# A hybrid convolution, attention and expert layer on one core: who scales the value rows, who sums the first norm, and in which order the head weights come

## The reference

```python
q, k = Wq @ x + bq, Wk @ x + bk           # 16 rows each
v = Wv @ x + bv                           # 128 rows
x = gamma * (v @ softmax(q.T @ k / 4).T) + x

t = tokens(x)
h = layernorm(t) @ qkv_w + qkv_b          # 8 heads, q and v of 128 each
attn = sum_n(q[:, n]) * sum_r(lunchbox)   # what the einsums come to, per head
t = t + (attn * v) @ proj_w + proj_b

t = t + moe(layernorm(t))                 # 8 experts, the best two of each token
```

## Time and profile before

| What | Value |
|---|---|
| Median of 3 executions | 491.35 us (491.24 to 493.74) |
| The profiled execution | 488.81 us |
| Its span, first to last instruction | 487.0 us |
| TensorE busy | 425.6 us, 87% |
| TensorE weight loads | 368.3 us, 76% |
| VectorE busy | 310.4 us, 64% |
| ScalarE busy | 197.5 us, 41% |
| GpSimd busy | 157.7 us, 32% |
| Mean granted clock of TensorE | 0.939 |

### The profile page before, as it was taken

One profiled execution on the slowest core, in us unless ns is written; L12 is line 12 of the kernel. 1 busy time (PEld: TensorE's weight loads), 2 busy tenths in 40 slices (PEclk: granted clock), 3 DMA queues, 4 the chain that ended last, 5 costly groups with the idle time before them and its releaser, 6 DMA issues.

```text
span 487.0 us, 9131 instructions
## 1 busy us (share of the span) xinstructions
PE 425.6 (87%) x2833; PEld 368.3 (76%) x2833; DVE 310.4 (64%) x834; ACT 197.5 (41%) x386; POOL 157.7 (32%) x163
## 2 busy tenths in 40 slices
PE   5989899999899988999879969986987999999825
PEld 2569567996669976778867969885876899999813
DVE  6855887458985589877667756744434455555425
ACT  4070534614337244163138336634333344444403
POOL 1020000010024440134517834455565444444510
PEclk9599999999999999999969979989899999999955
DMA  7090000100000200002103101123222222222159
GB/s 221 0 297 22 1 0 1 45 2 0 1 17 24 73 23 1 11 12 101 39 14 110 46 12 51 54 71 84 67 67 62 60 64 67 62 62 68 39 185 344
DMA packets 23621, 30.20 MB, mean 62 GB/s; under 512 B 5074, under 2 KB 16978, under 8 KB 23448
## 3 DMA queue, kind: packets, MB, share of 16 engines
q1 hardware_dynamic: 19256, 20.63, 14.2%
q0 software_dynamic: 4320, 8.99, 5.5%
HBM read 17.44 MB, written 12.16 MB: 61 GB/s over the span
## 4 chain that ended last, share of the span: by engine, by line
PE 60%; DVE 23%; issue 8%; ACT 5%; DMA 2%; POOL 0%; SPq 0%; another core or an unknown queue 0%; DVEq 0%; POOLq 0%; ACTq 0%
PE bank_c L393 27%; PE bank_s L393 21%; PE bank_c L592 4%; PE bank_a L393 4%; DVE row_max_sb L975 3%; DVE values_sb L1041 2%; DVE probs_sb L1422 2%; ACT probs_sb L804 2%; PE bank_a L571 1%; DVE ln_sb L1013 1%; DVE qk_sum_sb L1215 1%; DMA probs_sb<-y_dram 1%; DVE lnT_lo_sb L1210 1%; DVE qk_hi_sb L1220 1%; PE bank_a L464 1%
## 5 line engine op out<-in xcount | busy, mean ns | idle before, releaser
L1492 POOL DMA_INDIRECT y_dram<-probs_sb x71 | 68.2, 961 | 86.9 <-ACT probs_sb L914 84.3
L1447 POOL DMA_INDIRECT xs_dram<-ln_rows_sb,slots_sb x64 | 67.3, 1052 | 86.6 <-issue 57.4
L393 PE MATMUL bank_c<-v_ext_sb,probs_sb 128*128 128x129 f32 x512 | 61.4, 275 | 1.8 <-DVE t_sb L998 1.6
L847 ACT ACTIVATE values_sb<-bank_s,g_head_sb 128x1024 fp32r<-128x1024 f32 x32 | 35.1, 1113 | 66.0 <-PE bank_s L393 52.5
L393 PEld LDWEIGHTS bank_c<-v_ext_sb,probs_sb 128*128 128x128 f32 x512 | 59.4, 191 | 3.0 <-DVE t_sb L998 1.2
L393 PE MATMUL bank_s<-probs_sb,lnT_hi_sb 128*128 x142 | 52.9, 373 | 1.9 <-issue 1.3
L393 PE MATMUL bank_c<-values_sb,wp_hi_sb 128*128 128x256 f32 x256 | 53.8, 288 | 0.0
L1439 POOL TENSOR_TENSOR rstd_sb<-var_eps_sb,minus_half_sb 128x4 f32<-128x4 f32 x16 | 16.5, 1029 | 102.4 <-DVE var_eps_sb L1007 102.4
L1215 DVE TENSOR_TENSOR qk_sum_sb<-v_ext_sb,bank_s 128x341 f32<-128x341 f32 x35 | 17.8, 510 | 49.5 <-ACT v_ext_sb L903 31.9
L393 PE MATMUL bank_s<-w_rest_sb,lnT_hi_sb 128*128 x142 | 46.6, 328 | 0.0
L393 PE MATMUL bank_s<-probs_sb,lnT_lo_sb 128*128 x142 | 46.4, 327 | 0.0
(11 more groups left out here) (197 smaller groups left out, 899.5 us busy)
## 6 DMA issues: line engine op xcount, KB each, us to landing
probs_sb<-xs_dram SPq DMA_DIRECT2D x71, 66.0 KB
probs_sb<-y_dram SPq DMA_DIRECT2D x16, 256.0 KB, 6.7
w_rest_sb<-in_w_dram SPq DMA_DIRECT2D x1, 2728.0 KB, 13.8
xc_sb<-in_x_dram SPq DMA_DIRECT2D x4, 512.0 KB, 3.6
y_dram<-probs_sb POOLq DMA_INDIRECT x71
xs_dram<-ln_rows_sb,slots_sb POOLq DMA_INDIRECT x64
xs_dram<-pads_sb SPq DMA_DIRECT2D x1, 528.0 KB, 7.4
xs_dram<-pads_sb SPq DMA_DIRECT2D x8, 66.0 KB
```

The lines of the kernel that those rows point to most:

```text
L393: return nc.tensor.matmul(bank, lhsT, rhs, start=start, stop=stop)
L847: nc.scalar.activation(vh_hi[:, hd % RING, :], bank_s[hd % 2][:, :], ACT.Copy, scale=g_head[:, hd:hd + 1]).then_inc(vh_high, 1)
L1447: G.indirect_dma_start(xs_dram, bass.IndirectOffsetOnAxis(ap=slots[:, i, k:k + 1], axis=0), ln2x(i)[:, k // TILES, k % TILES, :], None).th ...
L1492: G.indirect_dma_start(y_dram, bass.IndirectOffsetOnAxis(ap=x_rows[k][:, C:C + 1].bitcast(I32), axis=0), y_rows[k], None).then_inc(scatter ...
```

## The change

It does four things. The value rows of images 1 to 3 are kept by ScalarE, which multiplies by gamma alone; their bias is added by TensorE, as one more matmul per half at the head of the accumulation, from 32 rows of the bias split into high and low parts (`bv_rows`) against rows that hold 1/16 (`shares`). The sum of the norm over tokens is made by TensorE: each of the eight tiles of normed rows stands as the stationary operand against a column of ones of `v_ext`, accumulated in one column of `bank_s[1]`, from which ScalarE copies it; the two accumulating reads of ScalarE go, and a bank `Cb` is drained by VectorE's low part. TensorE's `head_sums` stands ahead of head values 0, with one column where there were two, and VectorE's head weights stand between the query stack and the key stack, with three operations for four. Four small operations of VectorE are added ahead of the loop.

```diff
@@ TensorE
             def project_v(i, h):
+                if i == 1:
+                    pe.wait_ge(consts_made, 9)
                 pe.wait_ge(A[h].drained, A[h].before(i, "v"))
+                mm(bank_a[h][:, :], shares[BIAS_ROWS, :], bv_rows[BIAS_ROWS, :].unsqueeze(1).broadcast_to([2 * DQK, 4, C]), stop=False)
                 for j in range(4):
                     n = 4 * h + j
-                    last = mm(bank_a[h][:, j * C:(j + 1) * C], xc[:, n * P:(n + 1) * P], wvT_s[:])
+                    last = mm(bank_a[h][:, j * C:(j + 1) * C], xc[:, n * P:(n + 1) * P], wvT_s[:], start=False, stop=(j == 3))
                 last.then_inc(A[h].filled, 1)
...
+            def sum_ln1(i, h):
+                if h == 0:
+                    pe.wait_ge(S[1].drained, S[1].before(i, "sum"))
+                for n in range(4 * h, 4 * h + 4):
+                    last = mm(bank_s[1][:, 0:1], ln1[:, n, :], v_ext[:, 0, C:VCOLS], start=(n == 0), stop=(n == TILES - 1))
+                if h == 1:
+                    last.then_inc(S[1].filled, 1)
+
             def head_sums(i):
 
-                for h in range(2):
-                    pe.wait_ge(Cb[h].drained, Cb[h].after(i, "ln1"))
+                pe.wait_ge(S[1].drained, S[1].after(i, "sum"))
+                pe.wait_ge(Cb[0].drained, Cb[0].after(i, "ln1"))
                 for hd in range(HEADS):
-                    last = mm(bank_c[0][:, 2 * hd:2 * hd + 2], wq_s[:, hd * P:(hd + 1) * P], ln1_sum[:, :])
+                    last = mm(bank_c[0][:, hd:hd + 1], wq_s[:, hd * P:(hd + 1) * P], ln1_sum[:, :])
...
                     if hd == 0 and n == 2:
-                        pe.wait_ge(lnT_low, 2 * i + 2)
+                        for c in Cb:
+                            pe.wait_ge(c.drained, c.after(i, "ln1"))
...
                 turn_ln1(i, 0)
+                sum_ln1(i, 0)
                 if not last:
                     project_v(i + 1, 0)
                 if not first:
                     rank(i - 1)
                 turn_ln1(i, 1)
+                sum_ln1(i, 1)
                 if not last:
                     project_v(i + 1, 1)
...
+                head_sums(i)
                 head_values(i, 0)
-                head_sums(i)
                 head_values(i, 1)
@@ ScalarE
-                for h in range(2):
-                    act.wait_ge(lnT_low, 2 * i + h + 1)
-                    nc.scalar.activation(lnT[:, h * HALF:(h + 1) * HALF], bank_c[h][:, :], ACT.Identity,
-                                         accum_out=ln1_sum[:, h:h + 1]).then_inc(Cb[h].drained, 1)
+                act.wait_ge(S[1].filled, S[1].full(i, "sum"))
+                nc.scalar.copy(ln1_sum[:], bank_s[1][:, 0:1]).then_inc(S[1].drained, 1)
+
+            def keep_v(i):
+                for h in range(2):
+                    act.wait_ge(A[h].filled, A[h].full(i, "v"))
+                    nc.scalar.activation(v_ext[:, 4 * h:4 * h + 4, 0:C], bank_a[h][:, :].rearrange("p (n c) -> p n c", c=C),
+                                         ACT.Copy, scale=vec_s[:, 1:2]).then_inc(A[h].drained, 1)
...
                 keep_ln1T(i)
+                if not last:
+                    keep_v(i + 1)
                 keep_head_values(i)
@@ VectorE
             def head_weights(i):
                 s0 = i * G_STEPS
                 dve.wait_ge(Cb[0].filled, Cb[0].full(i, "qsum"))
-                V.tensor_reduce(qsum[:], bank_c[0][:, 0:2 * HEADS].rearrange("p (h t) -> p h t", t=2), AX_X, ALU.add).then_inc(Cb[0].drained, 1)
+                V.tensor_tensor(qsum[:], bank_c[0][:, 0:HEADS], nbq[:], ALU.add).then_inc(Cb[0].drained, 1)
                 dve.wait_ge(Cb[0].drained, Cb[0].after(i, "qsum"))
-                step(V.tensor_tensor(qsum[:], qsum[:], nbq[:], ALU.add), g_step, s0, 1)
-                step(V.tensor_scalar(g_head[:], qsum[:], lunch_sum[:, 0:1], None, ALU.mult), g_step, s0, 2)
+                step(V.tensor_scalar(g_head[:], qsum[:], lunch_sum[:, 0:1], None, ALU.mult), g_step, s0, 1)
...
-                    make_stacks(i + 1)
+                    make_stacks(i + 1, [QUERIES])
                 head_weights(i)
                 if not last:
-                    keep_v(i + 1)
+                    make_stacks(i + 1, [KEYS])
...
+            bv_hi = t1[BIAS_ROWS, TILES - 1, :].bitcast(F32R)
+            V.tensor_copy(bv_hi, bvB_s[BIAS_ROWS, :]).then_inc(setup, 1)
+            V.memset(shares[BIAS_ROWS, :].bitcast(F32), 1.0 / DQK).then_inc(consts_made, 1)
+            dve.wait_ge(setup, 5)
+            V.scalar_tensor_tensor(out=bv_rows[BIAS_ROWS, :], in0=bv_hi.bitcast(F32),
+                                   scalar=cst_s[BIAS_ROWS, C_LOW:C_LOW + 1],
+                                   in1=bvB_s[BIAS_ROWS, :],
+                                   op0=ALU.mult, op1=ALU.add).then_inc(consts_made, 1)
```

More of the change, by code:

```diff
@@ L124, in conv_attn_moe_kernel @@
         gbv = sb("gbv", [P, C])
+        BIAS_ROWS = slice(STACK, STACK + 2 * DQK)
+        bv_rows = sb("bv_rows", [P, C], F32R)
+        shares = sb("shares", [P, P], F32R)
         v_ext = sb("v_ext", [P, TILES, VCOLS])
@@ L147, in by_stride @@
             return half[:].rearrange("c (k p) -> c p k", k=HEADS)[:, h * (P // 2):(h + 1) * (P // 2), :]
-        ln1_sum = sb("ln1_sum", [P, 2])
+        ln1_sum = sb("ln1_sum", [P, 1])
         nbq = sb("nbq", [P, HEADS])
@@ L247, in order_s @@
             for i in range(IMAGES):
-                order += [("rank", i - 1, 0)] * (i > 0 and b == 0) + [("vh", i, k) for k in range(HEADS // 2)]
+                order += [("rank", i - 1, 0)] * (i > 0 and b == 0) + [("sum", i, 0)] * (b == 1) + [("vh", i, k) for k in range(HEADS // 2)]
                 if i + 1 < IMAGES:
@@ L277, in conv_attn_moe_kernel @@
         setup, den_ready, tok_step = sem("setup"), sem("den_ready"), sem("tok_step")
-        heads_made, vh_high, lnT_high, lnT_low = sem("heads_made"), sem("vh_high"), sem("lnT_high"), sem("lnT_low")
+        heads_made, vh_high, lnT_high = sem("heads_made"), sem("vh_high"), sem("lnT_high")
         qk_high, wv_low = sem("qk_high"), sem("wv_low")
         wv_high, g_step, bias_ready = sem("wv_high"), sem("g_step"), sem("bias_ready")
-        G_STEPS = 3
+        G_STEPS = 2
         tables_ready, table_step, hidden_cleared = sem("tables_ready"), sem("table_step"), sem("hidden_cleared")
@@ L836, in keep_ln1T @@
                     nc.scalar.copy(by_stride(lnT_hi, h), bank_c[h][:, :].rearrange("c (p k) -> c p k", k=HEADS)).then_inc(lnT_high, 1)
+                act.wait_ge(S[1].filled, S[1].full(i, "sum"))
+                nc.scalar.copy(ln1_sum[:], bank_s[1][:, 0:1]).then_inc(S[1].drained, 1)
+            def keep_v(i):
                 for h in range(2):
[L838 to L840 removed]
+                    act.wait_ge(A[h].filled, A[h].full(i, "v"))
+                    nc.scalar.activation(v_ext[:, 4 * h:4 * h + 4, 0:C], bank_a[h][:, :].rearrange("p (n c) -> p n c", c=C),
+                                         ACT.Copy, scale=vec_s[:, 1:2]).then_inc(A[h].drained, 1)
             def keep_head_values(i):
[L843 removed]
+                act.wait_ge(g_step, i * G_STEPS + 1)
                 for hd in range(HEADS):
@@ L956, in bcast_e, with make_stacks @@
                 return ap.unsqueeze(2).broadcast_to([P, TILES, EXPERTS])
-            def make_stacks(i):
+            QUERIES, KEYS = (q_stack, 0), (k_stack, STACK)
+            def make_stacks(i, stacks):
                 for h in range(2):
                     dve.wait_ge(A[h].drained, A[h].after(i, "qk"))
-                for k, (dst, lo) in enumerate(((q_stack, 0), (k_stack, STACK))):
+                for dst, lo in stacks:
                     rows = slice(lo, lo + STACK)
@@ L964, in make_stacks @@
                                            in1=qk_sum[rows, :], op0=ALU.mult, op1=ALU.add).then_inc(stack_step, 1)
-            def keep_v(i):
-                for h in range(2):
[L968 to L971, removed]
             def keep_max(i, n):
@@ L1035, in low_lnT @@
                     V.tensor_tensor(by_stride(lnT_lo, h), bank_c[h][:, :].rearrange("c (p k) -> c p k", k=HEADS),
-                                    by_stride(lnT_hi, h).bitcast(F32), ALU.subtract).then_inc(lnT_low, 1)
+                                    by_stride(lnT_hi, h).bitcast(F32), ALU.subtract).then_inc(Cb[h].drained, 1)
             def low_head_values(i, hd):
@@ L1350, in _ @@
             dve.wait_ge(qk_high, 2)
-            make_stacks(0)
+            make_stacks(0, [QUERIES, KEYS])
             for n in range(TILES):
```

## The result

The changed kernel takes 493.75 us in the median of 22 executions (490.90 to 496.98), the kernel before 491.06 (486.04 to 495.10) in the same session: a ratio of 1.0088, interval 1.0056 to 1.0119. Ratios and intervals leave out the executions more than 1.5% above the fastest of their kernel, here 5 of the 22 of the kernel before and none of the changed kernel's; over all executions the means are 490.45 and 493.64 us, a ratio of 1.0065. Forecast were 489.7 and a range of 487.0 to 492.2. The profiled execution took 494.10 us.

What follows compares the result with a forecast made beforehand. The bound was taken as the chain from the second turned half to low part 0, 7.74 us, held by VectorE. Terms -(0.58 - 0.19) - 0.58 - 0.58 - 0.1 = -1.65 us gave 489.7 us against the median, range 487.0 to 492.2.

Steps and rivals of the forecast that it cites:

- The clock in the first three images: Sum assumed 2.4 GHz around the query sums; rival: clock falls there, 2.5 us an image, 497.2 us, chance 0.08.
- The last image: Last image at half clock, up to ScalarE's high part behind head values 0: 255.4 against 255.50, so -0.1 us.
- The sum at full clock: Terms of the first three images at 2.4 GHz: -(0.58 - 0.19), -0.58 and -0.58 us, from low part 0 coming earlier.
- The narrow matmuls: Norm sum on TensorE: eight one-column matmuls per half at 0.111 us, 0.89 us; rival of cheap ones: 487.65 us, chance 0.05.
- The bias matmul: One fp32r matmul of 512 columns per half on TensorE: 0.24 us, upper bound 0.48 us giving a sum of -0.45.
- the distance: From the second turned half to low part 0 in the first three images: 7.16 us against 7.74.
- the turned half is late: Second turned half delayed by work added ahead on TensorE: 0.19 us in the first image, none in second and third.
- ScalarE's part: ScalarE swaps two accumulating reads for two value halves and a copy, done before head values 0 are full: zero.
- the key stack: VectorE's key stack, 1.28 us, moves behind the head weights and ends before the first row scores can start: zero.
- the setup: Four small operations ahead of the loop, under 1 us together, where VectorE idles 5.02 us: zero.
- SyncE: SyncE's list is as before; its third load of expert weights goes out about 2 us earlier, without a waiter.
- The rival of the full clock in the last image: Clock stays at 2.4 GHz through the last image, low part 0 2.75 us earlier: -4.3 us, 487.05 us, chance 0.15.

Runs made afterwards that it cites:

- b0: The kernel before, unchanged, run again as a kernel of its own; ratio to the kernel before 0.9966.
- r1: The changed kernel with its bias matmul over 128 rows, zeros outside the 32; one execution, 488.51 us.
- w2: The changed kernel with the sum of the norm in 128 columns and the query sums in 64 per head, second run; ratio to before 0.9987.
- a1: The changed kernel again, unchanged, in one session with w2, v1 and x1; ratio to before 1.0121.
- x1: The changed kernel without bias matmul, value rows kept by VectorE ahead of the head weights, norm sum and query sums wide; ratio to before 0.9978.
- v1: The changed kernel without bias matmul, value rows kept by VectorE ahead of the head weights, sums left narrow; ratio to before 1.0073.
- w1: Same kernel as w2, first run: changed kernel, norm sum in 128 columns, query sums in 64 per head; ratio to before 0.9973.
- x2: x1 plus two useless f32 matmuls of 512 columns behind the first turned half of the last image; ratio to before 0.9811.
- x3: x2 plus one useless 256-column f32 matmul behind each of the first image's six middle row scores; ratio to before 0.9868.
- x4: The same kernel as x2, run again; ratio to before 0.9834.
- f1: The kernel before plus three useless f32 matmuls of 512 columns behind the first turned half of the last image; ratio to before 0.9872.
- f4: The same kernel as f1, run again; ratio to before 0.9921.

## Why the prediction was wrong

**The clock in the first three images** is the first step that failed. The sum took 2.4 GHz for the changed stretch there, and a fall had a chance of 0.08. The mechanism of that rival was put as it came: narrow work around little wide work, a fall within it, head values 0 at half. So was its price, 2.5 us an image, 1.6 to 2.7 measured. What failed is the weight. "It held 2.4 GHz in these images" was read from one profile, in which there was one narrow group and head values 0 stood ahead of it. Another profile of the same kernel (b0) has a fall in the third image, at 185.7 us. In the changed kernel's profiles it fell in 4 of 12 images (7 of 15 with r1), so not in each. The Trainium skill's rule ("TensorE: Matmul & The Clock Gate", "HAM oscillation — how this bites in real kernels") speaks of idle waits; here the clock fell with TensorE busy all the time, so the measurement goes further than the page. That narrow groups cost time by the clock is shown by w2 against a1 and x1 against v1, 4.8 and 3.1 us. That it is these three images that lose it is argued: v1's profile has no fall there, and its clock over all executions is as low as a1's.

**The last image**, forecast at -0.1 us: low part 0 comes 10.45 us behind the turned half in all five profiles of the narrow form without filling work, against 9.82 in the profile of the kernel before and 10.28 in b0's, where the stretch is at half clock from its start as here. So the term is +0.2 to +0.6 us. The half clock lasts 10.2 or 13.7 us in both kernels, so a longer one is not shown.

**The sum at full clock** is the second step that failed, forecast at -0.39, -0.58, -0.58: the intervals show about 0, -0.2 and 0. The narrow matmuls (0.11 us an instruction) and their place were right, against the 25 ns that the Trainium skill ("TensorE: Matmul & The Clock Gate", "Back-to-back issue gap") gives. The bias matmul was mis-sized: 0.42 us for 0.24, and 0.99 us for 0.91 for the value half behind it, twice an image; its own upper bound of 0.48 us, with a sum of -0.45, was the nearer. So the distance is 7.33 to 7.39 for 7.16, and the turned half is late by 0.4, 0.2 and 0.1 us for 0.19, 0 and 0. Without that matmul the intervals are 0.5 and 0.6 us shorter than before (v1, x1), about the gain forecast, from another form. In means it weighs more, 3.6 us (a1 less v1) or 1.9 (w2 less x1), than the 1.5 us of the intervals; why is open.

**Right:** ScalarE's part (its value halves are done before the query sums end), the key stack, the setup, SyncE, and that TensorE's order and not VectorE's sets low part 0.

The rival of the full clock in the last image (0.15) came in w1 and w2 in part and in x2, x3, x4, f1 and f4 in full, and in no profile of the changed kernel. Not settled: what share of the 2.7 to 5 us is falls in the first three images, what the last, and what the extra fall of the start (2.4 us where it comes); the clock difference carries 1.7 of 3.5 and 3.2 of 5.0 us, and the clock is taken over the whole kernel.

## What to carry to other kernels

When a change adds narrow matmuls or moves them next to one another, do not take the clock of the old profile for the new stretch, even where TensorE stays busy. The test is cheap: give the same instructions more columns. Eight matmul instructions whose time is their weight load took 0.88 us with one column and 0.98 with 128, and with both groups widened the kernel became 4.8 us faster. A gap ahead of a dense stretch can be worth filling with useless wide matmuls, as f1 and f4 show (0.987 and 0.992, the filling work alone; x2 and x4, at 0.981 and 0.983, have other edits too). The matmul over 32 rows was not cheaper here than the same over 128, but 0.1 us dearer. And where executions of one kernel are spread over 6 us or more, read the granted clock of each before believing two profiles, and look where in the kernel it was lost.

## What the runs showed of the hardware that I had not expected

The clock fell with TensorE busy for 10.00 of 10.00 us and its weight loads for 8.46. An fp32r matmul of 32 rows and 512 columns stands 0.42 us ahead of the f32 matmul behind it, one of 128 rows 0.32, while fp32r matmuls among their like stand 0.24 apart. Behind the 32-row matmul the next weights are not loaded ahead, behind the 128-row one they are, which accounts for the 0.1 us. The Trainium skill ("TensorE: Matmul & The Clock Gate", "LDWEIGHTS (loading the stationary operand)") has a load of 32 rows take as long as one of 128; the trace agrees, with 0.18 and 0.19 us. Why the next load waits was not tried further.
